# A decoder's cross-attention values for two units at a time, self-attention blocks at the ends of units, and column sums in 32-column tiles

## The chip, the cores and the metric

The kernel runs on one core of a Trainium2 chip. The metric is the device time of one execution in microseconds (us), from the first to the last instruction. TensorE (PE in the profile, with its weight loads as PEld) multiplies, VectorE (DVE) and ScalarE (ACT) take results out of the accumulation banks (PSUM) and do the softmax and the norms, GpSimd (POOL) does one small power operation per norm, and SyncE (SP) issues the transfers. The engines wait for each other through semaphores.

## What is computed

The reference is a chain of twelve residual blocks over `x` of 32 sequences x 32 tokens x 256 features, with a context of 32 x 257 x 256. The change touches one of them, a decoder of six layers, here cut to its core:

```
for l in range(6):
    h = layer_norm(h + mha(h, h, sa_w[l], sa_b[l], mask))       # self-attention, 16 heads of 16
    h = layer_norm(h + mha(h, ctx, ca_w[l], ca_b[l], None))     # cross-attention, 257 keys
    h = layer_norm(h + relu(h @ w1[l] + b1[l]) @ w2[l] + b2[l]) # 256 -> 1024 -> 256
```

`mha` is q, k, v projections, softmax(q k / 4) v, and an output projection.

## The kernel before

All data is float32. The decoder (`decoder_layers`) treats four sequences of 32 tokens as one tile of 128 rows: eight tiles in each of six layers make 48 positions. It runs as a software pipeline of 51 **steps**; in step s, position s is in self-attention (jobs S0 to S7), position s-1 in preparation (n, q, K, V and, once in a layer, X), position s-2 in cross-attention, and position s-3 in the output projection (Y) and the feed-forward part (D0 to D3).

A step has eight **units**, 0 to 7, called u0 to u7 below. A cross-attention unit k is one sequence and one half of the heads. In unit `it` of the loop, TensorE does, in this order:

- `scores(it)`, L2274: four matmuls in tiles of 32 rows x 64 columns of the array, 257 columns each. It waits until ScalarE has taken the exponentials of the unit before (there is one pair of score banks).
- `transposes(it-1)`, L2282: four 128x128 transposes of the probabilities.
- the **jobs** of the unit, from the hand-written table `UNIT_JOBS` (L2052): projections and the like, nearly all full 128x128 matmuls. Job n goes into one of four ring banks and so waits until the result of job n-4 has been taken out.
- `values(it-2)`, L2294: eight matmuls of 64 columns in tiles of 128 rows x 32 columns. After the last sequence of a half there follow the **sums** (L2299), two matmuls of 256 columns in tiles of 64 columns; they come at the end of u1 and u5.

Two jobs are in 32-column tiles like the values: S3 (L2238, self-attention scores, first job of u3, eight matmuls of 256 columns) and S6 (L2246, self-attention values, first job of u6, 32 matmuls of 64 columns).

VectorE has its own list in each unit: first the score maxima (L2369), then the results of those jobs that are marked "dve", then at fixed units the softmax sums and their spreading (L2373 to L2375, u0 and u4), the selection of the own heads after the sums (L2386 to L2390, u1 and u5), the query blocks (L2395, u2), the self-attention softmax (L2403 to L2405 in u3, L2409 to L2412 in u4), and the last half of a norm (L2331 to L2333). The result of D3 is put off: it is taken in the next unit, behind the maxima. ScalarE takes exponentials (L2490), copies transposed probabilities to `pT` (L2495, two buffers) and takes the results of the jobs marked "act".

A job is called by its name and its line: n, S0 and D0 are L2199; q, S1q and S1k are L2206; K is L2213; V is L2219; Y is L2228; S2 is L2232; S7 is L2251; D1 and D2 are L2258; D3 is L2263. V5 means the sixth V job of a step, K5 the sixth K job.

Of the kernel before, what the change touches and what calls it, by code (L numbers as in the profile page):

```python
# [19 lines left out]
P = 128  # L20
NB = 32
LQ = 32
LK = 257
D = 256
DC = D // P
GB = P // LQ
# [2011 lines left out]
def decoder_layers(E, A):  # L2038

    nc, ps = E.nc, E.ps  # L2040
# [5 lines left out]
    def k_job(i):  # L2046
        return ("K", (i // GB, i % GB), "act")

    def v_job(i):
        return ("V", i, "dve")  # L2050
# [1 line left out]
    UNIT_JOBS = [  # L2052
        [k_job(0), v_job(0), k_job(1), v_job(1), ("S0", None, "act")],
        [("S1q", None, "dve"), k_job(2), ("S1k", None, "act"), k_job(3), ("n", None, "act")],
        [("q", None, "act"), k_job(4), ("Y", None, "dve")],
        [("S3", None, "dve"), k_job(5), v_job(2), k_job(6)],
        [("D0", None, "act"), v_job(3), v_job(4), v_job(5)],
        [("S2", None, "dve"), ("D1", 0, "act"), k_job(7), v_job(6)],
        [("S6", None, "dve"), ("D2", 1, "act"), v_job(7), ("X", None, "act")],
        [("S7", None, "dve"), ("D3", None, "dve")],  # L2060
    ]
    PART = {"n": "prep", "X": "prep", "q": "prep", "K": "prep", "V": "prep", "Y": "out", "S0": "sa", "S1q": "sa", "S1k": "sa", "S2": "sa", "S3": "sa", "S6": "sa", "S7": "sa",
# [11 lines left out]
    with ExitStack() as st:  # L2074
# [4 lines left out]
        def sb(name, shape):  # L2079
            return st.enter_context(nc.sbuf_tensor(f"layers_{name}", [P] + shape, F32))  # L2080

        nT, qT, qblk = sb("nT", [DC, P]), sb("qT", [DC, P]), sb("qblk", [2, DC, GB, 2 * LQ])
        KT, V = sb("KT", [2, DC, CT]), sb("V", [2, VC, D])
        probs, pT = sb("probs", [DC, GB, 2, LK]), sb("pT", [2, 2, KC, P])
        negmax, totals, spread = sb("negmax", [2, 2]), sb("totals", [2, 2, GB]), sb("spread", [2, 2, GB, LQ])
        blend, attnT = sb("blend", [2, GB, LQ]), sb("attnT", [DC, P])
        rates, last_v = sb("rates", [2, 2, GB]), sb("last_v", [2, DC, NB])
# [34 lines left out]
        def need(eng, name, n):  # L2122
            if n > 0:
                eng.wait_ge(s[name], n)
# [8 lines left out]
        def ca_unit(it):  # L2133
            pos = it // U - 2
            if not 0 <= pos < NPOS:
                return None
            return it - 2 * U, pos, it % U // GB, it % GB
# [8 lines left out]
        with nc.Block(no_gpsimd_drain=True) as blk:  # L2146
# [40 lines left out]
            def _(pe):  # L2187
# [97 lines left out]
                def values(k, pos, cc, j):  # L2285
                    tile = pos % NG
                    need(pe, "copied", k + 1)
                    if j == 0:
                        need(pe, "heads_ready", k // GB)
                        if cc == 0:  # L2290
                            need_evacuated(pe, pos, "V", VC - 1)
                    for c in range(KC):
                        for i in range(4):
                            last = mm(ps[32 * i:32 * (i + 1), PV, j * 64:(j + 1) * 64], V[:, pos % 2, KC * j + c, cc * P + 32 * i:cc * P + 32 * (i + 1)], pT[:, k % 2, i // 2, c, 64 * (i % 2):64 * (i % 2 + 1)], start=c == 0, stop=c == KC - 1)  # L2294
                    last.then_inc(s["pv_done"], 1)
                    if j == GB - 1:
                        pe.wait_ge(s["spread_ready"], k // GB + 1)
                        for t in range(2):
                            last = mm(ps[64 * t:64 * (t + 1), PV, D:2 * D], E.c("headcol"), spread[:, t].rearrange("p s j q -> p (s j q)"), start=True, stop=True)  # L2299
                        last.then_inc(s["shares_done"], 1)  # L2300

                for it in range(N * U):
                    if ca_unit(it):
                        scores(*ca_unit(it))
                    if ca_unit(it - 1):
                        transposes(*ca_unit(it - 1))
                    for a in jobs_in(it):
                        job(*a)
                    if ca_unit(it - 2):
                        values(*ca_unit(it - 2))  # L2310

            @blk.vector
            def _(dve):
# [102 lines left out]
                for it in range(N * U + 1):  # L2416
                    step, u = it // U, it % U
                    if ca_unit(it):
                        maxima(*ca_unit(it))
                    for a in put_off:  # L2420
                        take(*a)
                    put_off.clear()
                    for a in jobs_in(it):
                        if a[3] == "D3":
                            put_off.append(a)
                        else:
                            take(*a)
                    if ca_unit(it - 1):
                        if (it - 1) % GB == GB - 1:
                            reciprocals(*ca_unit(it - 1))  # L2430
                    if ca_unit(it - 2) and (it - 2) % GB == GB - 1:
                        own_heads(*ca_unit(it - 2))
                    if u == 2 and steps[step]["prep"] is not None:
                        own_queries(steps[step]["prep"])
                    if u == 3 and steps[step]["sa"] is not None:
                        self_shift(steps[step]["sa"])
                    if u == 4 and steps[step]["sa"] is not None:
                        self_shares(steps[step]["sa"])
                    for a in unfinished:
                        norm_apply(*a)  # L2440
                    unfinished.clear()
# [10 lines left out]
            @blk.scalar  # L2452
            def _(act):
                a = nc.scalar.activation

                def take(n, step, u, kind, arg, engine):
                    if engine != "act":
                        return
                    o = ps[:, RING + n % RB]
                    pos = steps[step][PART[kind]]  # L2460
                    act.wait_ge(s["job_done"], n + 1)
                    if kind in ("n", "S0", "D0"):
                        dst = {"n": nT, "S0": sa_nT, "D0": dm_nT}[kind]
                        last = nc.scalar.copy(dst[:].rearrange("p c t -> p (c t)"), o[:, 0:D])  # L2464
                    elif kind == "K":
                        m, j = arg
                        last = a(KT[:, pos % 2, m, j * LK:(j + 1) * LK], o[:, 0:LK], ACT.Identity, bias=ca_bk[:, m:m + 1])  # L2467
                    elif kind == "q":
                        for m in range(DC):
                            last = a(qT[:, m], o[:, m * P:(m + 1) * P], ACT.Identity, bias=ca_bq[:, m:m + 1])  # L2470
                    elif kind == "X":
                        need(act, "heads_ready", DC * (pos - NG))
                        for m in range(DC):
                            last = a(last_v[:, pos // NG % 2, m], o[:, m * NB:(m + 1) * NB], ACT.Identity, bias=ca_bv[:, m:m + 1])
                    elif kind == "S1k":
                        for m in range(DC):
                            last = a(sa_k[:, m], o[:, m * P:(m + 1) * P], ACT.Identity, bias=sa_cols[:, 2 + m:3 + m])
                    else:
                        for i in range(4):
                            m = 4 * arg + i  # L2480
                            last = a(hid[:, m], o[:, i * P:(i + 1) * P], ACT.Relu, bias=dm_cols[:, m:m + 1])  # L2481
                    last.then_inc(s["evac_act"], 1)

                def exponentials(k, pos, cc, j):
                    act.wait_ge(s["max_ready"], k + 1)
                    need(act, "transposed", k - U + 1)
                    if j == 0:
                        need(act, "spread_ready", k // GB - 1)
                    for t in range(2):
                        a(probs[:, cc, j, t], ps[:, t, 0:LK], ACT.Exp, bias=negmax[:, k % 2, t:t + 1], accum_out=totals[:, cc, t, j:j + 1]).then_inc(s["exp_done"], 1)  # L2490

                def copy_transposed(k, pos, cc, j):
                    act.wait_ge(s["transposed"], k + 1)
                    need(act, "pv_done", k - 1)
                    nc.scalar.copy(pT[:, k % 2].rearrange("p t c x -> p (t c x)"), ps[:, TURN]).then_inc(s["copied"], 1)  # L2495

                for it in range(N * U):
                    step, u = it // U, it % U
                    if ca_unit(it):
                        exponentials(*ca_unit(it))  # L2500
                    if ca_unit(it - 1):
                        copy_transposed(*ca_unit(it - 1))
                    for b in jobs_in(it):
                        take(*b)
                    if steps[step]["sa"] is not None and u == 3:
                        act.wait_ge(s["shifted"], steps[step]["sa"] + 1)
                        a(sa_sc[:], sa_sc[:], ACT.Exp).then_inc(s["soft_done"], 1)
# [1163 lines left out]
```

## Time and profile before

| what | value |
|---|---|
| median of 3 runs | 4630.01 us (4628.66 to 4630.09) |
| span of the profiled execution | 4633.9 us |
| PE busy over the span | 4098.1 us (88%) |
| DVE, ACT, POOL busy | 2617.3, 1862.2, 302.9 us |
| the decoder's steps | from about 732 to about 2890 us |
| one regular step | 43.58 us |

The page of the profile gives shares of the whole span. What a change inside the decoder is worth is read from the timeline of single steps: one row stands for consecutive instructions of one kind, with its start, the time to the end of its last instruction, the line, what it writes and reads, and how many. A row's length overlaps the next row, since matmuls are pipelined; what a block costs is the start of the next block minus its own start. The profile shows two records for each float32 matmul (one for each transpose), so eight matmuls are "x16". All regular steps repeat each other to 0.01 us; six of them, one in each layer, are longer by the job X.

### The profile page before, as it was taken

The page shows a single profiled execution, that of the slowest core. Times are in us where ns is not written, and L with a number is a line of the kernel's source. Part 1 is how long each engine was busy: PE and PEld are TensorE (multiplying, and loading weights), DVE is VectorE, ACT ScalarE, POOL GpSimd, SP SyncE. Part 2 cuts the span into 40 slices and gives each one's busy share as a digit, 9 for nine tenths or more (in the row PEclk, how much of TensorE's full clock was granted, in tenths as well). Part 3 has the DMA queues.
Part 4 walks back from the last instruction along what each step waited for, and adds up shares of the span by engine and source line. Part 5 has one row for each costly group of instructions (what it writes and reads, how often), then busy time and mean ns, then how long its engine had stood idle before and what let it go on. Part 6 is the DMA issues. An engine that isn't in the chain of part 4 may idle for free. (4 is left out here: it accounts for less than half of the span.)

```text
span 4633.9 us, 104319 instructions
## 1 busy us (share of the span) xinstructions
PE 4098.1 (88%) x43458; PEld 3113.7 (67%) x43458; DVE 2617.3 (56%) x5580; ACT 1862.2 (40%) x5080; POOL 302.9 (7%) x560
## 2 busy tenths in 40 slices
PE   7988995999999999999999997779588787888867
PEld 6766884777777777777777775568445477566635
DVE  3445115777777777777777774631367654345545
ACT  2221222444444444444444443312266454255523
POOL 0000001000000000000000000020211000000000
PEclk9998998999999999999999998879799788888878
DMA  4110572011111111111101100038544300000000
GB/s 146 59 57 10 189 290 98 29 41 33 50 41 34 50 35 39 50 30 44 50 29 46 50 29 9 3 148 299 172 152 144 107 8 0 24 28 28 11 1 12
DMA packets 116917, 310.49 MB, mean 67 GB/s; under 512 B 29352, under 2 KB 75624, under 8 KB 92016
## 3 DMA queue, kind: packets, MB, share of 16 engines
q1 hardware_dynamic: 113392, 295.61, 18.7%
q0 software_dynamic: 3072, 8.39, 0.5%
q8 instruction: 339, 5.55, 0.5%
q14 instruction: 114, 0.93, 0.1%
HBM read 289.01 MB, written 14.94 MB: 66 GB/s over the span
## 5 line engine op out<-in xcount | busy, mean ns | idle before, releaser
L2490 ACT ACTIVATE layers_probs<-banks,layers_negmax 128x257 f32<-128x257 f32 x768 | 358.3, 472 | 1004.4 <-DVE layers_negmax L2369 1004.4
L2213 PE MATMUL banks<-ctx_tiles,weights_a 128*128 128x257 f32 x1536 | 401.6, 384 | 0.0
L2219 PE MATMUL banks<-weights_a,ctx_tiles 128*128 128x256 f32 x1536 | 378.9, 379 | 0.0
L2219 PEld LDWEIGHTS banks<-weights_a,ctx_tiles 128*128 128x128 f32 x1536 | 284.5, 190 | 35.3
L2369 DVE TENSOR_REDUCE layers_negmax<-banks 128x2 f32<-128x514 f32 x384 | 262.6, 684 | 70.5 <-PE banks L2274 70.5
L2213 PEld LDWEIGHTS banks<-ctx_tiles,weights_a 128*128 128x128 f32 x1536 | 270.4, 191 | 45.6 <-issue 18.9
L2349 DVE TENSOR_TENSOR layers_V<-banks,rows_a 128x256 f32<-128x256 f32 x384 | 160.6, 419 | 191.2 <-PE banks L2219 185.3
L2274 PE MATMUL banks<-layers_KT,layers_qblk 32*64 32x257 f32 x3072 | 256.0, 403 | 10.8 <-ACT layers_probs L2490 8.0
L2282 PEld LDWEIGHTS banks<-const,layers_probs 128*128 128x128 f32 x1536 | 162.3, 142 | 149.3 <-issue 149.2
L2282 PE MATMUL banks<-const,layers_probs 128*128 128x128 f32 x1536 | 253.3, 288 | 0.0
L2495 ACT COPY layers_pT<-banks 128x512 f32<-128x512 f32 x384 | 223.7, 582 | 3.3 <-PE banks L2282 3.3
L2467 ACT ACTIVATE layers_KT<-banks,layers_ca_bk 128x257 f32<-128x257 f32 x384 | 184.6, 497 | 46.3 <-PE banks L2213 46.2
L2258 PE MATMUL banks<-layers_dm_nT,weights_b 128*128 128x128 f32 x1536 | 193.9, 280 | 0.6 <-ACT layers_dm_nT L2464 0.6
L2258 PEld LDWEIGHTS banks<-layers_dm_nT,weights_b 128*128 128x128 f32 x1536 | 184.7, 194 | 7.4 <-ACT layers_dm_nT L2464 0.9
L2294 PEld LDWEIGHTS banks<-layers_pT,layers_V 128*32 128x32 f32 x6144 | 103.7, 109 | 110.5 <-issue 108.6
L2263 PE MATMUL banks<-weights_b,layers_hid 128*128 128x256 f32 x768 | 173.7, 379 | 1.7 <-ACT layers_hid L2481 1.7
L2294 PE MATMUL banks<-layers_pT,layers_V 128*32 128x64 f32 x6144 | 165.8, 225 | 0.3 <-ACT layers_pT L2495 0.3
L2263 PEld LDWEIGHTS banks<-weights_b,layers_hid 128*128 128x128 f32 x768 | 145.7, 190 | 21.7 <-issue 2.1
L2490 ACT ACTIVATION_READ_ACCUMULATOR layers_probs<-banks,layers_negmax 128x1 f32 x768 | 150.4, 196 | 0.0
L2274 PEld LDWEIGHTS banks<-layers_KT,layers_qblk 32*64 32x64 f32 x3072 | 79.5, 130 | 78.1 <-issue 36.5
L2772 PE MATMUL banks<-weights_a,ctx_tiles 128*128 128x512 f32 x256 | 131.2, 642 | 0.5
L2345 DVE SCALAR_TENSOR_TENSOR weights_a<-banks,layers_sa_cols,const 128x1024 f32<-128x1024 f32 x96 | 118.4, 1275 | 5.9 <-PE banks L2206 5.9
(695 smaller groups left out, 8350.7 us busy)
## 6 DMA issues: line engine op xcount, KB each, us to landing
ctx_tiles<-in_ctx SPq DMA_DIRECT2D x65, 1028.0 KB, 5.0
weights_a<-in_L_w SPq DMA_DIRECT2D x44, 1024.0 KB, 6.8
l2x_B<-positions SPq DMA_DIRECT2D x32, 1280.0 KB, 5.9
weights_b<-in_L_w SPq DMA_DIRECT2D x32, 1024.0 KB
weights_c<-in_L_w SPq DMA_DIRECT2D x16, 1024.0 KB
weights_b<-in_L_xattn_w SPq DMA_DIRECT2D x12, 1024.0 KB, 6.2
l0x_key_rows<-in_ctx_rows SPq DMA_DIRECT2D x32, 256.0 KB, 2.6
ctx_tiles<-in_ctx_keys SPq DMA_DIRECT2D x32, 256.0 KB, 2.7
```

Of the source, the lines that this page charges most:

```text
L2213: last = mm(o[:, 0:LK], ca_wk[:, c, m * P:(m + 1) * P], E.ctx[:, tile % 2, c, j * LK:(j + 1) * LK], start=c == 0, stop=c == DC - 1)
L2219: last = mm(o[:, 0:D], E.ctx[:, tile % 2, c, first:first + P], ca_wv[:, c], start=c == 0, stop=c == DC - 1)
L2258: last = mm(o[:, i * P:(i + 1) * P], dm_w1[:, c, m * P:(m + 1) * P], dm_nT[:, c], start=c == 0, stop=c == DC - 1)
L2263: last = mm(o[:, 0:D], hid[:, m], dm_w2[:, m], start=m == 0, stop=m == FC - 1)
L2274: last = mm(ps[half, r // 2, 0:LK], qblk[rows, tile % 2, cc, j], KT[rows, tile % 2, cc, j * LK:(j + 1) * LK], start=True, stop=True)
L2282: last = tr(ps[:, TURN, (KC * t + c) * P:(KC * t + c + 1) * P], probs[:, cc, j, t, 1 + c * P:1 + (c + 1) * P], E.c("ident"))
L2294: last = mm(ps[32 * i:32 * (i + 1), PV, j * 64:(j + 1) * 64], V[:, pos % 2, KC * j + c, cc * P + 32 * i:cc * P + 32 * (i + 1)], pT[:, k % ...
L2349: last = v.tensor_tensor(V[:, tile % 2, arg], o[:, 0:D], E.rA[:, 0], ALU.add)
L2369: v.tensor_reduce(negmax[:, k % 2], ps[:, 0:2, 0:LK], AX.X, ALU.max, negate=True).then_inc(s["max_ready"], 1)
L2467: last = a(KT[:, pos % 2, m, j * LK:(j + 1) * LK], o[:, 0:LK], ACT.Identity, bias=ca_bk[:, m:m + 1])
L2490: a(probs[:, cc, j, t], ps[:, t, 0:LK], ACT.Exp, bias=negmax[:, k % 2, t:t + 1], accum_out=totals[:, cc, t, j:j + 1]).then_inc(s["exp_done ...
L2495: nc.scalar.copy(pT[:, k % 2].rearrange("p t c x -> p (t c x)"), ps[:, TURN]).then_inc(s["copied"], 1)
```

## The change

Four things change in `decoder_layers`.

1. `values` is called only in odd units, for two units one after the other (it-3, then it-2). `pT` gets four buffers instead of two, and ScalarE's copy waits for values two units further back.
2. S3 becomes the last job of u2 instead of the first of u3, and S6 the last of u5 instead of the first of u6.
3. VectorE puts off S3 and S6 as it did D3, so it takes them in the unit after.
4. The sums become four matmuls in 32-column tiles, each with half of the columns of the constant, instead of two in 64-column tiles.

```
-        [("q", None, "act"), k_job(4), ("Y", None, "dve")],
-        [("S3", None, "dve"), k_job(5), v_job(2), k_job(6)],
+        [("q", None, "act"), k_job(4), ("Y", None, "dve"), ("S3", None, "dve")],
+        [k_job(5), v_job(2), k_job(6)],
         [("D0", None, "act"), v_job(3), v_job(4), v_job(5)],
-        [("S2", None, "dve"), ("D1", 0, "act"), k_job(7), v_job(6)],
-        [("S6", None, "dve"), ("D2", 1, "act"), v_job(7), ("X", None, "act")],
+        [("S2", None, "dve"), ("D1", 0, "act"), k_job(7), v_job(6), ("S6", None, "dve")],
+        [("D2", 1, "act"), v_job(7), ("X", None, "act")],
...
-        probs, pT = sb("probs", [DC, GB, 2, LK]), sb("pT", [2, 2, KC, P])
+        probs, pT = sb("probs", [DC, GB, 2, LK]), sb("pT", [4, 2, KC, P])
...
-                        for t in range(2):
-                            last = mm(ps[64 * t:64 * (t + 1), PV, D:2 * D], E.c("headcol"), spread[:, t].rearrange("p s j q -> p (s j q)"), start=True, stop=True)
+                        for i in range(4):
+                            last = mm(ps[32 * i:32 * (i + 1), PV, D:2 * D], E.c("headcol")[:, 32 * (i % 2):32 * (i % 2 + 1)], spread[:, i // 2].rearrange("p s j q -> p (s j q)"), start=True, stop=True)
...
-                    if ca_unit(it - 2):
-                        values(*ca_unit(it - 2))
+                    for back in (3, 2):
+                        if it % 2 and ca_unit(it - back):
+                            values(*ca_unit(it - back))
...
-                        if a[3] == "D3":
+                        if a[3] in ("S3", "S6", "D3"):
...
-                    need(act, "pv_done", k - 1)
-                    nc.scalar.copy(pT[:, k % 2].rearrange("p t c x -> p (t c x)"), ps[:, TURN]).then_inc(s["copied"], 1)
+                    need(act, "pv_done", k - 3)
+                    nc.scalar.copy(pT[:, k % 4].rearrange("p t c x -> p (t c x)"), ps[:, TURN]).then_inc(s["copied"], 1)
```

Only TensorE's order changes. VectorE, ScalarE, GpSimd and SyncE have the same instructions in the same order as before, S3 and S6 included, since what VectorE puts off lands where it stood; only ScalarE's copies (L2495) lose a wait at the first units.

On TensorE from the end of u1 to u3, before (values and sums, scores, transposes, q, K4, Y, values, scores, transposes, S3, K5):

```order
L2294 MATMUL banks<-layers_pT,layers_V 32x64 x8
L2299 MATMUL banks<-layers_spread,const 64x256 x2
L2274 MATMUL banks<-layers_KT,layers_qblk 64x257 x4
L2282 MATMUL banks<-const,layers_probs 128x128 x4
L2206 MATMUL banks<-layers_nT,weights_a 128x128 x4
L2213 MATMUL banks<-ctx_tiles,weights_a 128x257 x2
L2228 MATMUL banks<-weights_a,layers_attnT 128x256 x2
L2294 MATMUL banks<-layers_pT,layers_V 32x64 x8
L2274 MATMUL banks<-layers_KT,layers_qblk 64x257 x4
L2282 MATMUL banks<-const,layers_probs 128x128 x4
L2238 MATMUL banks<-weights_a,layers_sa_k 32x256 x8
L2213 MATMUL banks<-ctx_tiles,weights_a 128x257 x2
```

And after:

```order
L2294 MATMUL banks<-layers_pT,layers_V 32x64 x16
L2299 MATMUL banks<-layers_spread,const 32x256 x4
L2274 MATMUL banks<-layers_KT,layers_qblk 64x257 x4
L2282 MATMUL banks<-const,layers_probs 128x128 x4
L2206 MATMUL banks<-layers_nT,weights_a 128x128 x4
L2213 MATMUL banks<-ctx_tiles,weights_a 128x257 x2
L2228 MATMUL banks<-weights_a,layers_attnT 128x256 x2
L2238 MATMUL banks<-weights_a,layers_sa_k 32x256 x8
L2274 MATMUL banks<-layers_KT,layers_qblk 64x257 x4
L2282 MATMUL banks<-const,layers_probs 128x128 x4
L2213 MATMUL banks<-ctx_tiles,weights_a 128x257 x2
```

The values behind Y are gone (they stand at the end of u3, with those of the unit after), and S3 stands in their place; K5 follows the transposes directly.

On TensorE from V6 at the end of u5 into u6, before:

```order
L2219 MATMUL banks<-weights_a,ctx_tiles 128x256 x2
L2294 MATMUL banks<-layers_pT,layers_V 32x64 x8
L2299 MATMUL banks<-layers_spread,const 64x256 x2
L2274 MATMUL banks<-layers_KT,layers_qblk 64x257 x4
L2282 MATMUL banks<-const,layers_probs 128x128 x4
L2246 MATMUL banks<-layers_sa_pT,layers_sa_v 32x64 x32
L2258 MATMUL banks<-layers_dm_nT,weights_b 128x128 x8
```

And after:

```order
L2219 MATMUL banks<-weights_a,ctx_tiles 128x256 x2
L2246 MATMUL banks<-layers_sa_pT,layers_sa_v 32x64 x32
L2294 MATMUL banks<-layers_pT,layers_V 32x64 x16
L2299 MATMUL banks<-layers_spread,const 32x256 x4
L2274 MATMUL banks<-layers_KT,layers_qblk 64x257 x4
L2282 MATMUL banks<-const,layers_probs 128x128 x4
L2258 MATMUL banks<-layers_dm_nT,weights_b 128x128 x8
```

S6 now stands ahead of the values, which are those of two units, and D2 follows the transposes directly.

## Rows read from the trace of the kernel before

**Rows 1.** One step: window, length, busy (count) of PE, PEld, DVE, ACT, POOL; clock, DMA

```profile
1528.28:1571.86 43.58, 43.02 (x468) 32.52 (x467) 31.49 (x70) 19.94 (x66) 2.48 (x6) 1.00 0.17 59
```

**Rows 2.** Timeline of PE, u5 into u7: start, length, line, operation, [idle before]

```profile
1539.04 0.43 PE L2294 MATMUL banks<-layers_pT,layers_V 128*32 128x64 f32 x16
...
1541.36 1.95 PE L2258 MATMUL banks<-layers_dm_nT,weights_b 128*128 128x128 f32 x16
1543.14 1.03 PE L2213 MATMUL banks<-ctx_tiles,weights_a 128*128 128x257 f32 x4
1544.01 1.03 PE L2219 MATMUL banks<-weights_a,ctx_tiles 128*128 128x256 f32 x4
...
1544.97 0.43 PE L2294 MATMUL banks<-layers_pT,layers_V 128*32 128x64 f32 x16
1545.33 0.65 PE L2299 MATMUL banks<-layers_spread,const 128*64 128x256 f32 x4
1545.91 0.66 PE L2274 MATMUL banks<-layers_KT,layers_qblk 32*64 32x257 f32 x8
...
1547.09 1.10 PE L2246 MATMUL banks<-layers_sa_pT,layers_sa_v 128*32 128x64 f32 x64
1548.12 2.05 PE L2258 MATMUL banks<-layers_dm_nT,weights_b 128*128 128x128 f32 x16
1550.01 1.03 PE L2219 MATMUL banks<-weights_a,ctx_tiles 128*128 128x256 f32 x4
...
1551.33 0.66 PE L2274 MATMUL banks<-layers_KT,layers_qblk 32*64 32x257 f32 x8
```

**Rows 3.** L2294 alone in 0.02 us of the block at 1544.97: PE, PEld; clock

```profile
1545.17:1545.19 0.02, 0.02 (x16) 0.02 (x6) 1.00 0.00 0
```

**Rows 4.** Timeline of PE while the pipeline fills: n, then scores without values between

```profile
784.08 0.44 PE L2199 MATMUL banks<-const,h_state 128*128 128x128 f32 x2 [1.76 <-ACT layers_KT L2467]
784.45 0.66 PE L2274 MATMUL banks<-layers_KT,layers_qblk 32*64 32x257 f32 x8
```

**Rows 5.** Timeline of PE, u2 to u4 of the same step

```profile
1528.28 1.03 PE L2228 MATMUL banks<-weights_a,layers_attnT 128*128 128x256 f32 x4
1529.23 0.43 PE L2294 MATMUL banks<-layers_pT,layers_V 128*32 128x64 f32 x16
...
1530.77 1.07 PE L2238 MATMUL banks<-weights_a,layers_sa_k 128*32 128x256 f32 x16
1531.77 1.13 PE L2213 MATMUL banks<-ctx_tiles,weights_a 128*128 128x257 f32 x4
...
1534.57 0.43 PE L2294 MATMUL banks<-layers_pT,layers_V 128*32 128x64 f32 x16
1535.05 0.66 PE L2274 MATMUL banks<-layers_KT,layers_qblk 32*64 32x257 f32 x8
```

**Rows 6.** Timelines of DVE and ACT, u2 and u3: Y's result, the last exponential

```profile
1529.34 0.42 DVE L2320 TENSOR_TENSOR layers_y_ca<-banks,rows_a 128x256 f32<-128x256 f32 x1 [1.53 <-PE banks L2228]
...
1534.80 0.20 ACT L2490 ACTIVATION_READ_ACCUMULATOR layers_probs<-banks,layers_negmax 128x1 f32 x1
```

**Rows 7.** Timeline of DVE, u4 and u5: V5's result, and S2's

```profile
1539.15 0.43 DVE L2349 TENSOR_TENSOR layers_V<-banks,rows_a 128x256 f32<-128x256 f32 x1 [0.44 <-PE banks L2219]
...
1543.47 1.21 DVE L2351 TENSOR_TENSOR layers_sa_v<-banks,const 128x1024 f32<-128x1024 f32 x1
```

**Rows 8.** Timelines of DVE and PE, u0 and u1: V1's result, S1q's, and n

```profile
1561.94 0.42 DVE L2349 TENSOR_TENSOR layers_V<-banks,rows_a 128x256 f32<-128x256 f32 x1 [1.30 <-PE banks L2219]
...
1565.17 2.47 DVE L2345 SCALAR_TENSOR_TENSOR weights_a<-banks,layers_sa_cols,const 128x1024 f32<-128x1024 f32 x2
...
1567.69 0.44 PE L2199 MATMUL banks<-const,h_state 128*128 128x128 f32 x2 [0.51 <-DVE weights_a L2345]
```

**Rows 9.** Waits from 860 to 2780 us: who for whom, total us, times, longest

```profile
PE banks L2199 <- DVE weights_a L2345: 22.4, 44, 0.5
```

**Rows 10.** Timeline of ACT, u6: end of its exponentials

```profile
1549.15 0.20 ACT L2490 ACTIVATION_READ_ACCUMULATOR layers_probs<-banks,layers_negmax 128x1 f32 x1
```

More of the change, by code:

```diff
@@ L2293, in values @@
                         for i in range(4):
-                            last = mm(ps[32 * i:32 * (i + 1), PV, j * 64:(j + 1) * 64], V[:, pos % 2, KC * j + c, cc * P + 32 * i:cc * P + 32 * (i + 1)], pT[:, k % 2, i // 2, c, 64 * (i % 2):64 * (i % 2 + 1)], start=c == 0, stop=c == KC - 1)
+                            last = mm(ps[32 * i:32 * (i + 1), PV, j * 64:(j + 1) * 64], V[:, pos % 2, KC * j + c, cc * P + 32 * i:cc * P + 32 * (i + 1)], pT[:, k % 4, i // 2, c, 64 * (i % 2):64 * (i % 2 + 1)], start=c == 0, stop=c == KC - 1)
                     last.then_inc(s["pv_done"], 1)
```

## Prediction

> **What bounds the kernel now.** I read the busy time of one step first, then the timeline of TensorE through it, and then who released each idle time. In a regular step TensorE is busy for 43.02 of 43.58 us, at a granted clock of 1.00 [rows 1]. So the step is TensorE's stream plus a little waiting, and the reader should look at what that stream spends between blocks. A values block (16 records) takes 0.36 us until the next block starts (1544.97 to 1545.33) [rows 2]. Yet 0.20 us after its start all 16 records are under way [rows 3], and nothing begins for the other 0.16. The block of 64 such records, S6, takes 1.03 us [rows 2]. The 48 more cost 0.67, or 14 ns each, so 16 records are worth 0.22 us and the way out of the tile shape costs 0.36 - 0.22 = 0.14, which I use as 0.15. The way in costs too: K7, followed by a job of the same shape, takes 0.87; V6, followed by values, 0.96 [rows 2], so 0.09. Behind S6 or S3 the next job is also late: D2 takes 1.89 us against 1.78 for D1 (1541.36 to 1543.14) [rows 2], another 0.11. A block of odd shape among full ones therefore costs some 0.25 to 0.35 us beside its work, and this is what the change can save.
>
> Three places in the step follow another engine, and there TensorE's work is not what counts. All three repeat in 44 steps; the first one is the wait counted 44 times [rows 9].
> - **n in u1** waits for the ring bank of S1q, which VectorE frees at 1565.17 + 2.47 = 1567.64; n starts at 1567.69, after 0.51 us idle [rows 8]. VectorE was last idle before V1's result (1561.94) and has worked without a gap since.
> - **scores in u4** wait for the exponentials of u3, which end at 1534.80 + 0.20 = 1535.00; the scores start at 1535.05, and the values block ahead of them lasts 0.48 instead of 0.36, so 0.12 us is waiting [rows 5, 6]. The chain began with Y's result at 1529.34 [rows 6].
> - **S6** needs S2's result, ready at 1543.47 + 1.21 = 1544.68, in a chain that began with V5's result at 1539.15 [rows 7]. S6 now comes at 1547.09 [rows 2] and never notices.
>
> **The change, stretch by stretch.** The other engines keep their order, so these chains keep their length, counted from the TensorE job that starts them.
>
> *V1 to n (u0, u1).* The values block of u0 (0.36 with its way out) leaves. It stood in front of a wait, so the wait only grows from 0.51 to 0.87 us: n starts just as late. Change 0. Scores directly behind a full job, which this adds in every even unit, need a way in as the values do; where the pipeline fills, such a pair is seen, n to scores in 0.37 us (784.08 to 784.45) [rows 4]. I price it like the 0.09 of V6 to values, so it cancels.
>
> *n to Y (u1, u2).* Before: values 0.36 and sums 0.58 (1545.33 to 1545.91) [rows 2], 0.94 in all. After: two values blocks 2 x 0.22, sums, one way out. For the sums in four tiles the nearest row is S3, also 256 columns in 32-column tiles: 16 records in 1.00 us [rows 5], less 0.15 is 0.85, and the sums have 8 records, so 0.43. Together 0.44 + 0.43 + 0.15 = 1.02. Change +0.08. If the four tiles did not overlap, the bound would be eight records at a quarter of 0.87, 1.7 us; S3 speaks against it, and I take 0.43.
>
> *Y to scores of u4.* Gone are the values of u2 (0.36), the way into S3 (0.09) and the delay behind it (0.11); a second block of values (0.22) comes in at the end of u3. TensorE would arrive at 1535.05 - 0.12 - 0.36 - 0.09 - 0.11 + 0.22 = 1534.59. The exponentials still end at 1535.00. Change 0, with a wait of 0.46 instead of 0.12. S3 itself keeps its 1.00 [rows 5], and its way in behind Y is the one that the values have there now (Y to values 0.95, against 0.87 for a full job) [rows 2, 5].
>
> *Scores of u4 to scores of u7.* Up to V5 nothing changes. Then the values of u4 (0.36) leave, so V6 ends at 1544.97 - 0.36 = 1544.61. S6 cannot start before 1544.68 + 0.05 = 1544.73 (the 0.05 from the n above): a new wait of 0.12. Then S6 without way out 0.88, two values blocks 0.44, sums 0.43, way out 0.15: scores of u6 at 1546.63. Scores and transposes took 1.18 with the way into S6 [rows 2], now 1.09: 1547.72. D2 takes 1.78 and V7 0.96: scores of u7 at 1550.46. Before it was 1551.33 [rows 2]. Change -0.87. The cover must hold at one more place: the exponentials of u6 now end 1549.35 - 1545.33 = 4.02 us after the sums start [rows 2, 10], and the scores of u7 will start 0.43 + 0.15 + 1.09 + 1.78 + 0.96 = 4.41 after it. So 0.39 us of slack is left; every tenth more that VectorE or ScalarE needs there is lost.
>
> *u7 to u0.* One more values block of 0.22 in u7. Change +0.22.
>
> The four `pT` buffers cost no time: the copy waits for values that are as far behind as before. No transfer is moved, and SP's and POOL's queues are untouched.
>
> **Sum.** 0 + 0.08 + 0 - 0.87 + 0.22 = -0.57 us a step, so 43.58 becomes about 43.0. Over 44 regular steps that is -25 us. The two filling and three emptying steps have only parts of the pattern; at the full rate they would give -3, where waits already bind nothing, and I take -2. The profiled execution, 4633.9 us, becomes about 4607, and the median, which stands 3.9 us below it, 4630.0 - 27 = 4603 us, 0.58% faster.
>
> **Rivals.**
> - *The waits do not bind.* If VectorE's chains gave way with TensorE, the waits would not grow by 0.36 + 0.34 + 0.12 = 0.82, the step would lose 1.39 us, and the time would be 4630 - 61 - 3 = 4566 us. For it: TensorE is 99% busy. Against it: all three chains run without idle time from a TensorE event whose place does not move. Chance 5%.
> - *The gaps belong to the blocks, not to the change of shape (slower).* If a values block takes 0.36 us wherever it stands, because its second half accumulates onto its first, a pair takes 0.72 and S6 keeps 1.03. Then n to Y is 0.72 + 0.58 - 0.94 = +0.36; u5 to u7 is -0.87 + (1.03 + 0.72 + 0.58 - 1.90) = -0.44; u7 is +0.36; sum +0.28 a step, 4642 us. It decides from a block cost of about 0.29 us, where the sum is zero. For it: S6 does not accumulate, values do. Against it: all 16 records have started after 0.20 us [rows 3]. Chance 7%. A rule of the Trainium skill stands near it ("TensorE: Matmul & The Clock Gate", in "Wait — 56ns, not 53.3ns?"): starts of matmuls never come closer than about 25 ns. By it 16 records need 0.40 us; the 64 records of S6 in 1.03 us, 16 ns each, disagree, unless it is meant for whole matmuls, of which there are half as many.
> - *One chain turns out later.* The slack of 0.39 us before the scores of u7, or of the exponentials of u4 before the scores of u5, is used up, or the new waits cost a restart of 0.1 each. That takes back 0.2 to 0.6 a step: 4612 to 4630 us. Chance 13%.
> - *More is saved inside the forecast's mechanism.* The way out counted at 0.17 instead of 0.15 and the sums better overlapped: up to -0.8 a step, 4593 us. This is part of the forecast's own range.
>
> **How the numbers follow.** The forecast has 75%; its own range is 4593 to 4612. The range of 4586 to 4620 takes in most of the case of a late chain, and leaves out the first two rivals. A measurement of this kernel can tell about 0.2% (9 us) from no change. Faster by more than that: the forecast, the first rival, and half of the third case, 86%. Within 0.2%: the other half and a third of the second rival, 8%. Slower: 6%.
>
> **What would show it.** In the profile after, a regular step should be 43.0 us; n should wait for L2345 by about 0.87 us, scores of u4 for exponentials by about 0.46, S6 for L2351 by about 0.1; a block of values x32 should take 0.44 before the sums and 0.59 before the scores; the sums 0.58 to the scores; K5 and D2 should have lost their 0.1 us. If x32 takes 0.7, the slower rival holds. If a wait before the scores of u7 or u5 appears, the third. The forecast fails if VectorE starts any of the three chains earlier than it does now.

## Result: 4609.7 us, 0.38% faster

The changed kernel takes 4609.69 us (median of 5 runs, 4606.42 to 4611.30) against 4628.66 (4623.20 to 4630.09) for the kernel before: a ratio of 0.9962, 95% interval 0.9951 to 0.9973. The forecast was 4603, in a range of 4586 to 4620. The profiled execution spans 4604.6 us.

The timeline of TensorE through one regular step, from Y to the next Y, in the kernel after (start, length, line, operation, idle before):

```profile
1514.21 1.03 PE L2228 MATMUL banks<-weights_a,layers_attnT 128*128 128x256 f32 x4
1515.16 1.07 PE L2238 MATMUL banks<-weights_a,layers_sa_k 128*32 128x256 f32 x16
1516.16 0.66 PE L2274 MATMUL banks<-layers_KT,layers_qblk 32*64 32x257 f32 x8
...
1519.94 0.65 PE L2294 MATMUL banks<-layers_pT,layers_V 128*32 128x64 f32 x32
1520.98 0.66 PE L2274 MATMUL banks<-layers_KT,layers_qblk 32*64 32x257 f32 x8 [0.39 <-ACT layers_probs L2491]
...
1530.71 1.10 PE L2246 MATMUL banks<-layers_sa_pT,layers_sa_v 128*32 128x64 f32 x64
1531.60 0.66 PE L2294 MATMUL banks<-layers_pT,layers_V 128*32 128x64 f32 x32
1532.05 0.64 PE L2299 MATMUL banks<-layers_spread,const 128*32 128x256 f32 x8
1532.62 0.66 PE L2274 MATMUL banks<-layers_KT,layers_qblk 32*64 32x257 f32 x8
1533.22 0.66 PE L2282 MATMUL banks<-const,layers_probs 128*128 128x128 f32 x4
1533.71 1.95 PE L2258 MATMUL banks<-layers_dm_nT,weights_b 128*128 128x128 f32 x16
1535.50 1.03 PE L2219 MATMUL banks<-weights_a,ctx_tiles 128*128 128x256 f32 x4
1536.45 0.66 PE L2274 MATMUL banks<-layers_KT,layers_qblk 32*64 32x257 f32 x8
...
1541.95 0.65 PE L2294 MATMUL banks<-layers_pT,layers_V 128*32 128x64 f32 x32
1542.54 0.66 PE L2274 MATMUL banks<-layers_KT,layers_qblk 32*64 32x257 f32 x8
...
1551.14 1.03 PE L2213 MATMUL banks<-ctx_tiles,weights_a 128*128 128x257 f32 x4
1553.04 0.44 PE L2199 MATMUL banks<-const,h_state 128*128 128x128 f32 x2 [0.87 <-DVE weights_a L2346]
1553.41 0.65 PE L2294 MATMUL banks<-layers_pT,layers_V 128*32 128x64 f32 x32
1553.88 0.61 PE L2299 MATMUL banks<-layers_spread,const 128*32 128x256 f32 x8
1554.42 0.66 PE L2274 MATMUL banks<-layers_KT,layers_qblk 32*64 32x257 f32 x8
...
1557.27 1.03 PE L2228 MATMUL banks<-weights_a,layers_attnT 128*128 128x256 f32 x4
```

A block of values for two units (x32) takes 0.59 us ahead of scores (1541.95 to 1542.54) and 0.45 to 0.47 ahead of the sums, where one unit (x16) took 0.36 [rows 2]. D2 behind the transposes takes 1.79 us, not 1.89. Two waits have grown. The idle time shown at n went from 0.51 [rows 8] to 0.87 us. At the scores of u4, 0.39 is shown; from start to start the values block ahead of them lasts 1.04 us instead of 0.59, so 0.45 is waiting, where it was 0.12 before [rows 5]. The whole step, and its stretches from the start of one block to the start of the next:

| stretch | before | after | change | forecast |
|---|---|---|---|---|
| Y to scores of u4 | 6.77 | 6.77 | 0.00 | 0 |
| scores of u4 to scores of u7 | 16.28 | 15.47 | -0.81 | -0.87 |
| scores of u7 to scores of u0 | 5.86 | 6.09 | +0.23 | +0.22 |
| scores of u0 to n | 10.50 | 10.50 | 0.00 | 0 |
| n to Y | 4.16 | 4.23 | +0.07 | +0.08 |
| step | 43.58 | 43.07 | -0.51 | -0.57 |

(The last row is the median over the regular steps; the five stretches of this one step add up to 43.57 and 43.06.)

S6 now waits for S2's result. VectorE's timeline in the kernel after has it here:

```profile
1529.40 1.21 DVE L2352 TENSOR_TENSOR layers_sa_v<-banks,const 128x1024 f32<-128x1024 f32 x1
```

It ends at 1530.61, and S6 starts at 1530.71. From the first to the 45th Y, 44 steps, the trace before counts 1921.47 us, the one after 1898.89: 22.6 us less.

### The profile page after: what moved, and what is told of

Read it like the earlier page. It is cut to its first block and busy times, and to the rows that moved or that the text cites. A ratio compares the mean times of both kernels' runs of the same rounds, so it can differ in the third digit from the quotient of the medians.

```text
span 4604.6 us, 105085 instructions
## 1 busy us (share of the span) xinstructions
PE 4033.4 (88%) x43842; PEld 3091.5 (67%) x43842; DVE 2612.7 (57%) x5580; ACT 1857.0 (40%) x5080; POOL 301.1 (7%) x560
## 5 line engine op out<-in xcount | busy, mean ns | idle before, releaser
L2199 PE MATMUL banks<-const,h_state 128*128 128x128 f32 x288 | 58.5, 285 | 78.6 <-DVE weights_a L2346 38.2
L2294 PE MATMUL banks<-layers_pT,layers_V 128*32 128x64 f32 x6144 | 125.9, 221 | 0.3 <-ACT layers_pT L2496 0.3
L2387 DVE TENSOR_SCALAR layers_blend<-banks,const 128x128 f32<-128x128 f32 x96 | 33.6, 350 | 162.3 <-PE banks L2299 160.5
```

## Experiments

**Theory**: a change of tile shape costs TensorE some 0.25 us, but three chains of VectorE decide how much of that reaches the end: V1 to S1q's result (for n), Y to the exponentials of u3 (for the scores of u4), V5 to S2's result (for S6). **Rival**: TensorE's stream sets the time, and the waits only show slack. In all results below, "step" is the median distance from one Y to the next in the profile, which repeats to 0.02 us in nearly all regular steps; a ratio is against the kernel before on the same chip, with its 95% interval.

### Each part of the change alone

Values of two units together, alone: `for back in (3, 2)` and four `pT` buffers, with `UNIT_JOBS`, the put-off results and the sums as before.

> The kernel before with the values of two units together alone (and four pT buffers); S3, S6 and the sums stay. Theory (three chains of VectorE hold n, the scores of u4 and, after the change, S6): the values taken out of u0 and u2 only lengthen waits, those added in u1 and u7 cost 0.22 us each, u4 to u6 lose 0.50: -0.06 us a step, a regular step of 43.52 us, 3 us in all, with the wait of n at 0.87 and that of the scores of u4 at 0.26. Rival (TensorE's stream sets the time): four changes of shape less, -0.56 us a step, step 43.0, 25 us in all.

Measured: step 43.53, ratio 0.9999 (0.9989 to 1.0009). Waits of this kernel over 860 to 2700 us (total, times, longest):

```profile
PE banks L2199 <- DVE weights_a L2346: 36.6, 42, 0.9
PE banks L2274 <- ACT layers_probs L2491: 8.3, 42, 0.2
```

36.6 / 42 = 0.87 for n. The 0.20 shown at the scores of u4 is 0.26 from start to start (the values block ahead of them lasts 0.85 us, not 0.59), as expected. Four changes of shape less in a step, and nothing comes out: the rival's 43.0 is excluded.

S3 and S6 moved alone:

```
-        [("q", None, "act"), k_job(4), ("Y", None, "dve")],
-        [("S3", None, "dve"), k_job(5), v_job(2), k_job(6)],
+        [("q", None, "act"), k_job(4), ("Y", None, "dve"), ("S3", None, "dve")],
+        [k_job(5), v_job(2), k_job(6)],
...
-                        if a[3] == "D3":
+                        if a[3] in ("S3", "S6", "D3"):
```

(and S6 likewise, from the head of u6 to the end of u5.)

> The kernel before with S3 and S6 moved to the ends of u2 and u5 alone; values stay in each unit. Theory: the 0.35 us around S3 goes into the wait of the scores of u4, which grows from 0.12 to 0.47; the 0.35 around S6 is saved, and S6 finds S2's result ready: step 43.23 us, 15 us in all. Rival (stream only): both count, step 42.88, 31 us in all.

Measured: step 43.25, ratio 0.9969 (0.9958 to 0.9980). The gain is S6's 0.33. S3's went into the wait of the scores of u4, now 0.39 us as shown and 0.46 from start to start (0.82 instead of 0.36 for the values block ahead of them):

```profile
PE banks L2274 <- ACT layers_probs L2490: 16.8, 43, 0.4
```

Sums in four 32-column tiles alone, `for i in range(4)` over `ps[32 * i:32 * (i + 1), ...]`:

> The kernel before with the sums in four tiles of 32 columns alone. Both theories: the way out of the values' shape before the sums goes, 0.15 us twice a step, step 43.28 us, 13 us in all. If the four matmuls did not overlap, +1.3 us twice, step 46 us.

Measured: step 43.28, ratio 0.9985 (0.9975 to 0.9994). Exactly 0.30 a step, and four tiles overlap as S3's do. Of the 0.15 at each place, 0.12 is the values block (0.24 us ahead of the sums instead of 0.36) and 0.03 the sums themselves (0.55 instead of 0.58).

The changed kernel without the pairing:

```
-                    for back in (3, 2):
-                        if it % 2 and ca_unit(it - back):
-                            values(*ca_unit(it - back))
+                    if ca_unit(it - 2):
+                        values(*ca_unit(it - 2))
```

> The changed kernel with the pairing of the values taken back (values in each unit, S3, S6 and sums as changed). Theory: -0.35 (S6) -0.30 (sums) = -0.65 us a step, step 42.93, which is 0.13 faster than the changed kernel's 43.07, with the waits at 0.51 (n), 0.47 (scores of u4) and none at S6: 29 us below the kernel before. Rival (stream only, pairing worth 0.56): step 43.07 + 0.56 = 43.6 us.

Measured: step 42.94, ratio 0.9961 (0.9947 to 0.9975). By the step it is 0.13 us shorter than the changed kernel's, 6 us over 44 steps; the total times cannot tell the two apart. So the pairing, which the title names first, gains 0.05 us a step alone and costs 0.13 on top of the other parts. The three parts alone sum to -0.05 - 0.33 - 0.30 = -0.68, and the whole gives -0.51. The missing 0.17 is S6's wait (V6 to S6 takes 1.13 us in the changed kernel), which needs two parts at once: S6 early, and the values of u4 gone from in front of it. TensorE's timeline without the pairing shows S6 entering without a wait, V6 to S6 in the usual 0.95:

```profile
1528.69 1.03 PE L2219 MATMUL banks<-weights_a,ctx_tiles 128*128 128x256 f32 x4
1529.64 1.10 PE L2246 MATMUL banks<-layers_sa_pT,layers_sa_v 128*32 128x64 f32 x64
1530.56 0.41 PE L2294 MATMUL banks<-layers_pT,layers_V 128*32 128x64 f32 x16
1530.79 0.61 PE L2299 MATMUL banks<-layers_spread,const 128*32 128x256 f32 x8
```

It also shows a single values block between two blocks of its own shape: 0.23 us (1530.56 to 1530.79) instead of 0.36. That is the change of shape measured by itself, 0.13 us.

### VectorE's chains shortened

In these every instruction is kept, and VectorE does three, six or nine of its instructions in a step later than before. TensorE's order is that of the kernel each is built on, except where the values are said to stand elsewhere. The feed-forward norm's second half (`norm_apply` of "dm") behind S1q's result in u1 instead of ahead of it in u0:

```
                     for a in jobs_in(it):
...
+                    if u == 1:
+                        finish("dm")
...
-                    for a in unfinished:
-                        norm_apply(*a)
-                    unfinished.clear()
+                    finish(*(k for k in ("ca", "sa", "dm") if k not in late))
```

(`finish` does the halves of the named norms that are still open; `late` names those that have a place of their own, here "dm".)

> The changed kernel, with the second half of the feed-forward norm (three VectorE instructions, 1.25 us) done behind S1q's result in u1 instead of ahead of it in u0. Nothing is removed. Theory (n waits for VectorE's chain): S1q's result is ready 1.25 us earlier, n waits for nothing, 0.87 us less a step: 42.2 us, 38 us below the changed kernel. Rival (TensorE's stream sets the time, the wait is only where its slack is shown): no change, 43.07.

Measured: step 42.15, ratio 0.9870 (0.9853 to 0.9886).

The cross-attention norm's second half in u3, `if u == 3: finish("ca")` behind the maxima and the put-off results, with `late = ("ca",)`:

> The changed kernel, with the second half of the cross-attention norm done in u3 behind the maxima and S3's result instead of in u2 ahead of them. Theory: the exponentials of u3 end 1.7 us earlier and the scores of u4 wait for nothing: 0.39 to 0.46 us less a step, 42.64 us. Rival: no change, or the work only moves into the self-attention softmax and comes out as a wait of the scores of u5: 43.07.

Measured: step 42.60, ratio 0.9912 (0.9893 to 0.9931).

Both:

> The changed kernel with both norms finished late. Theory: the two waits are independent, 42.2 - 0.43 = 41.8 us a step, about 57 us below the changed kernel and 77 below the kernel before (4547 us); S6's wait of 0.17 stays. Rival: one gain only, 42.2 to 42.6, with a new wait before the scores of u5 or u7.

Measured: step 41.68, ratio 0.9812 (0.9796 to 0.9829). 0.92 and 0.47 us alone, 1.39 together: the two are independent, and the rival is out. TensorE's timeline of this kernel, with both waits gone:

```profile
1529.79 1.03 PE L2213 MATMUL banks<-ctx_tiles,weights_a 128*128 128x257 f32 x4
1530.76 0.44 PE L2199 MATMUL banks<-const,h_state 128*128 128x128 f32 x2
...
1540.73 0.65 PE L2294 MATMUL banks<-layers_pT,layers_V 128*32 128x64 f32 x32
1541.31 0.66 PE L2274 MATMUL banks<-layers_KT,layers_qblk 32*64 32x257 f32 x8
```

K3 to n is 0.97 us here and 1.90 in the changed kernel (1551.14 to 1553.04), so the wait cost 0.93, not the 0.87 shown as idle; the shown idle time starts at a modelled end of the matmul before. The values ahead of the scores of u4 take 0.58 instead of 1.04, so that wait cost 0.46, not 0.39. The two sum to the 1.39 that was gained; the 41.8 expected took the wait of n at the 0.87 shown.

The same with the values in each unit:

> As the run before (both norms late), but with the values in each unit, not paired. This prices the pairing where no wait hides it. Theory: four ways out and in less, 0.14 us each, less S6's wait of 0.17: this kernel is slower than the paired one, 41.95 against 41.8 us a step, 7 to 15 us. Rival (pairing is worth nothing, as in the run of the pairing alone): both alike.

Measured: step 41.91, ratio 0.9833 (0.9817 to 0.9850). Now the pairing is worth 0.23 us a step, where before it cost 0.13. Three pairs save 0.13 each; the one of u2 and u3 saves nothing, since S3 already stands in front of the values of u2 in the same shape; S6's wait takes 0.17 back: 0.39 - 0.17 = 0.22. The expectation counted four pairs, which by its own terms is 4 x 0.14 - 0.17 = 0.39, and wrote a difference of 0.15; the 0.23 agrees with neither. The count of three is an explanation after the fact, but the two traces show it: the pairs of u4, u6 and u0 with the unit behind each save 0.12, 0.14 and 0.14 us, and from Y to the scores of u4 both kernels take 6.32.

The kernel before, with the same two edits:

> The kernel before with both norms late and nothing of the change. Theory: only its two waits go, 0.51 and 0.12, step 42.95 us, 28 us below the kernel before. Against the changed kernel with the same two edits (41.68) the change would then be worth 1.27 us a step instead of 0.51. Rival (the change is worth the same everywhere): 42.2.

Measured: step 42.88, ratio 0.9932 (0.9915 to 0.9950). The two waits cost 0.70 together (0.57 from start to start at n, 0.12 at the scores), and the step has no idle time of TensorE left (42.88 busy of 42.88 us). The change is thus worth 42.88 - 41.68 = 1.20 us a step once VectorE does not hold TensorE, and 0.51 as it was made.

The softmax sums of u4 behind S2's result in u5 (on top of both norms late):

```
                         else:
                             take(*a)
+                        if a[3] == "S2" and ca_unit(it - 2):
+                            reciprocals(*ca_unit(it - 2))
+                            done_at.append(it)
...
-                        if (it - 1) % GB == GB - 1:
+                        if u == 0:
                             reciprocals(*ca_unit(it - 1))
```

> The changed kernel with both norms late, and the softmax sums of u4 (three VectorE instructions, 1.04 us) done behind S2's result in u5 instead of behind V5's in u4. Theory: S2's result is ready 1.04 us earlier, S6 no longer waits (0.17), and the spread is still ready before the sums want it: 41.68 - 0.17 = 41.51 us a step, 7 us less. Rival: the sums become late and wait instead, no change or slower.

Measured: step 41.51, ratio 0.9798 (0.9782 to 0.9814). As expected to 0.01 us, and V6 to S6 is back at 0.96 us: S2's result was what S6 waited for. In the busy time of one step (window, length, then busy and count of PE, PEld, DVE, ACT, POOL, clock, DMA) TensorE has no idle time left, against 41.69 of 43.06 in the changed kernel, whose row stands second:

```profile
1494.85:1536.36 41.51, 41.51 (x475) 32.07 (x474) 31.40 (x70) 20.07 (x66) 2.48 (x6) 1.00 0.28 100
```

```profile
1514.21:1557.27 43.06, 41.69 (x475) 32.10 (x474) 31.41 (x70) 19.82 (x66) 2.48 (x6) 1.00 0.17 60
```

The same work on every engine, 1.55 us apart. It also gives the price of TensorE's order without any wait: 42.88 us for the kernel before with both norms late less 41.51 is 1.37, and the prediction had 0.57 + 0.82 = 1.39 for it.

The values of units 0 to 3 all at u5 (on top of that), `for back in {1: (3, 2), 5: (5, 4, 3, 2), 7: (3, 2)}.get(it % U, ())`:

> As the first of these three, and the values of units 0 to 3 all at u5 (six pT buffers), none in u3. One block less, the same matmuls. Theory (a way out of the shape costs 0.14 wherever it is and waits for nothing here): 41.51 - 0.14 = 41.37 us a step, 6 us less. Rival (the cost belongs to the matmuls): no change.

Measured: step 41.55, ratio 0.9797 (0.9781 to 0.9814). A miss by 0.18. TensorE's timeline:

```profile
1507.14 2.76 PE L2219 MATMUL banks<-weights_a,ctx_tiles 128*128 128x256 f32 x12
1510.00 0.66 PE L2274 MATMUL banks<-layers_KT,layers_qblk 32*64 32x257 f32 x8
...
1516.48 1.08 PE L2294 MATMUL banks<-layers_pT,layers_V 128*32 128x64 f32 x64
1517.38 0.61 PE L2299 MATMUL banks<-layers_spread,const 128*32 128x256 f32 x8
```

The four units take 0.90 us (1516.48 to 1517.38), twice a pair's 0.45, and the block of u3 is gone: 0.59 - 0.45 = 0.14 saved, as expected. But V3 to V5 and the scores of u5 behind them are now 2.86 us apart (1507.14 to 1510.00) instead of 2.68 (1502.48 to 1505.16 in the kernel it is built on). The scores of u5 wait these 0.18 us for the exponentials of u4, whose last one ends at 1509.95:

```profile
1509.75 0.20 ACT L2507 ACTIVATION_READ_ACCUMULATOR layers_probs<-banks,layers_negmax 128x1 f32 x1
```

That is 9.85 us after the start of Y, and it is 9.85 in the kernel it is built on too, where the scores of u5 came 0.46 us after it. So this chain is counted from Y like that of u3. The scores start 0.05 us behind it now, so there were 0.41 us of slack; the 0.59 taken out of u3 used them up and 0.18 more. It is the mistake of the change itself once more: work taken from in front of a wait. Five of this kernel's steps are also 0.1 to 1.1 us longer than the median; why was not tried.

## Why the prediction was right, and what was off

**Where the step goes** held stretch by stretch, to 0.01 us in four of five. The values of u0 and u2 vanished into the waits of n and of the scores of u4, and n's wait is the 0.87 that was worked out, that of the scores of u4 0.45 from start to start against 0.46.

**The price of a shape** held: 0.22 us of work and 0.14 of change in a values block. Taken apart directly it is 0.36 against 0.23 for a block that is followed by its own shape, and blocks of 16, 32 and 64 records ahead of their own shape take 0.23, 0.45 and 0.90 us. The slower rival wanted 0.72 for a pair ahead of scores; it is 0.59, and the rival is out. (Its own terms give a sum of zero at a block cost of 0.30 us, not 0.29; nothing hangs on it.) The Trainium skill names 25 ns between starts of matmuls in "TensorE: Matmul & The Clock Gate", section "Wait — 56ns, not 53.3ns?". Taken for the records of the profile, this case does not agree: S6's 64 records take 0.89 us with no change of shape behind them, 14 ns each. For whole matmuls of two records (28 ns) it is not contradicted.

**The other rivals.** The waits bind: with them the order is worth 0.51 us a step, without them 1.37. Of the third rival, a later chain, only a trace is seen: no wait stands before the scores of u5 or u7, but S6's costs 0.05 more than it was priced at.

**The term that was off** is u4 to u7, -0.81 instead of -0.87. S6 started 0.10 us after S2's result, not 0.05. The 0.05 was read from n, a transposition on full tiles; the cause of the difference was not tried. The rest of that stretch came out at 5.74 us against 5.73.

**The emptying steps** were priced at a gain, and in the profiled executions they show a loss. From the 45th Y to the last, 106.45 us before became 107.66: the first two of these three steps are 1.1 us shorter together, the last is 2.3 longer. In the last one (the same columns as above, before and then after), TensorE has nearly the same matmuls (the sums have more):

```profile
2827.74:2857.33 29.59, 22.77 (x255) 15.31 (x255) 13.54 (x35) 11.99 (x40) 2.07 (x4) 0.85 0.01 1
```

```profile
2798.17:2830.09 31.92, 23.55 (x264) 16.52 (x263) 13.53 (x35) 11.97 (x40) 2.06 (x4) 0.80 0.01 2
```

TensorE is busy for 0.8 us more and idle for 1.5 more, and the granted clock is 0.80 instead of 0.85 of full speed, so more of the step runs at the lower of the two levels. For the whole stretch the pairing alone has 106.44 us and the kernel without the pairing 105.52, so neither shows the loss by itself. With both norms late, the kernel before, the changed one, the one without the pairing and the one with the softmax sums late all have a clock of 0.98 to 1.00 in the last step, and it takes 25.5 to 25.8 us. These differences are larger than the one to be explained, and each kernel has one profiled execution. Why the clock was lower stays open.

**The filling steps**, from the decoder's first matmul to the first Y, took 97.0 us before and 101.5 after in the profiled executions, with a granted clock of 0.93 and 0.88. The kernel without the pairing has 101.5 too, the pairing alone 96.8. The prediction had a small gain here; what the change does to this stretch apart from the clock is not shown.

**Size.** The 44 steps gained 22.6 us by the traces, where 25 were forecast (the 0.06 of S6's stretch). The ends were to gain 2 and show a loss, 1.2 us in the emptying steps and 4.5 in the filling ones. The medians are 19.0 us apart, and the interval runs from 13 to 23 us. So the forecast of 27 was too large, and 4609.7 lies in its own range of 4593 to 4612 only near the end. That the profiled execution came out at 4604.6 us, close to the 4607 of the forecast, is luck: it reached the decoder's first matmul 10.3 us earlier than the execution before did, and nothing was changed ahead of it. The chance of 5% for "the waits do not bind" was, by the runs that shortened the chains, still generous.

## What to carry to other kernels

- Before pricing a saving on the busiest engine, find the places where it waits, however little, and follow each back to the event that starts its chain. Work removed between that event and the wait is worth nothing as long as there is a wait; here that held for more than half of what the change saved on TensorE (0.51 of 1.37 us a step reached the end).
- A short wait on an engine that is 97 to 99% busy can be the cheapest thing to fix. Three reorderings on VectorE, which remove no instruction, took away waits of 0.93, 0.46 and 0.17 us and were worth 1.55 us a step; with the change they give 0.9798 of the time before (0.9782 to 0.9814), against 0.9962 for the change alone.
- Parts of an edit interact through such waits: price the whole, not the parts, and look at what is late next.

## What the hardware showed that was not expected

- Leaving the 128x32 tile shape costs 0.11 to 0.14 us of TensorE time, whether a full 128x128 job comes next (S6, 1.03 against 0.89 or 0.92), scores in 32x64 tiles (values, 0.36 against 0.23) or sums in 64-column tiles (0.36 against 0.24). Entering it from full jobs costs 0.09, and a full job right behind S6 runs 0.10 us longer still (D2, 1.89 against 1.79). Between S3, values and sums, all in 128x32 tiles with different column counts, no such cost is seen.
- The idle time shown before an instruction understates a short wait of TensorE: 0.87 shown at n was 0.93 by starts, 0.51 was 0.57, and 0.39 at the scores of u4 was 0.46.
